# First attention of a decoder block: rotary products for head pairs, queries and keys in alternate slots

## What is computed

```
q, k, v = complex projections of x, 16 heads x 64
phase = cos(t*om) + i sin(t*om)         # om = [omega, -omega], 32 + 32 frequencies per head
qr, kr = q * phase, k * phase
s  = real(sum_d qr[i,d] * conj(kr[j,d]))
qn, kn = sum_d |q|^2, sum_d |k|^2
E  = exp(-mu * |i-j|)
maha = max(qn[i] + E^2*kn[j] - 2*E*s, 0) / V(E)
logits = coef * log1p(maha / nu) - 0.5*64*log(V), causal
out = softmax(logits) @ v ; y = [real(out), imag(out)] @ Wo
```

## Time and profile before

| | |
|---|---|
| median of 3 runs | 2667.71 us (2659.65 to 2667.91) |
| the profiled execution | 2664.52 us, of which the span of the core is 2662.8 us |
| PE busy | 2141.3 us (80%), 14544 products |
| DVE busy | 1698.4 us (64%) |
| ACT busy | 1213.7 us (46%) |
| POOL busy | 716.1 us (27%) |
| mean granted TensorE clock | 0.91 of full |
| chain that ended last | PE 43%, DVE 37%, issue 13%, ACT 4%, POOL 2% |

### The profile page before, as it was taken

How to read it: one execution, slowest core, us unless ns; L and a number is a source line. 1 busy time by engine, 2 the same in 40 slices (tenths; PEclk the granted TensorE clock), 3 DMA queues, 4 the chain that set the end, 5 groups by cost and what they waited for, 6 DMA issues and landing times.

```text
span 2662.8 us, 41353 instructions
## 1 busy us (share of the span) xinstructions
PE 2141.3 (80%) x14544; PEld 1454.7 (55%) x14544; DVE 1698.4 (64%) x3952; ACT 1213.7 (46%) x2950; POOL 716.1 (27%) x647
## 2 busy tenths in 40 slices
PE   2885888689887888679887888679887888688687
PEld 1554466546664566546664566546664566555344
DVE  8976972689346972679356972679346972623444
ACT  2551575246632574236632575236632574233233
POOL 0541540135201540135201540135201540100000
PEclk8996999899997999799997999899987999788799
DMA  4000000000000000000000000000000000020000
GB/s 173 1 2 15 1 1 9 1 17 1 9 1 2 17 1 9 1 18 1 9 1 2 17 1 9 1 18 1 9 1 2 17 1 9 1 79 1 9 16 16
DMA packets 17371, 33.08 MB, mean 12 GB/s; under 512 B 2735, under 2 KB 8887, under 8 KB 16391
## 3 DMA queue, kind: packets, MB, share of 16 engines
q1 hardware_dynamic: 15718, 25.61, 2.8%
q0 software_dynamic: 1440, 4.72, 0.5%
HBM read 24.03 MB, written 5.77 MB: 11 GB/s over the span
## 4 chain that ended last, share of the span: by engine, by line
PE 43%; DVE 37%; issue 13%; ACT 4%; POOL 2%; DVEq 0%; ACTq 0%; SPq 0%; DMA 0%; POOLq 0%
PE bank L1138 41%; DVE work L414 11%; DVE bank L423 5%; DVE work L412 3%; DVE work L432 3%; ACT work L788 2%; PE bank L1142 2%; DVE max L655 2%; POOL work L1048 1%; POOL work L1060 1%; DVE norm_x_st L357 1%; DVE act_row L367 1%; POOL work L1055 1%; DVE acc L578 1%; DVE negmax L434 1%
## 5 line engine op out<-in xcount | busy, mean ns | idle before, releaser
L1138 PEld LDWEIGHTS bank<-work 128*128 128x128 f32 (+2 forms) x5152 | 377.0, 190 | 182.9 <-issue 155.6
L1138 PE MATMUL bank<-work 128*128 128x128 f32 (+2 forms) x5152 | 407.1, 296 | 64.7 <-DMA work<-in_wo 34.7
L788 ACT ACTIVATE work<-bank 128x512 f32<-128x512 f32 (+1 forms) x560 | 244.6, 516 | 260.6 <-PE bank L1138 246.6
L414 DVE TENSOR_TENSOR work<-bank,table_space 64x512 f32<-64x512 f32 x512 | 352.1, 688 | 6.8
L1138 PEld LDWEIGHTS bank<-sb_w_down,hid 128*128 128x128 f32 x2304 | 287.9, 198 | 89.1 <-issue 52.3
L1138 PE MATMUL bank<-act_T,sb_w_up 128*128 128x512 f32 x576 | 292.6, 631 | 33.9 <-ACT hid L788 18.9
L788 ACT ACTIVATE hid<-bank,sb_b_up 128x512 f32<-128x512 f32 x288 | 193.3, 686 | 252.8 <-PE bank L1138 246.7
L1138 PE MATMUL bank<-sb_w_down,hid 128*128 128x128 f32 x2304 | 289.9, 281 | 16.8 <-DVE acc L578 16.8
L578 DVE SCALAR_TENSOR_TENSOR acc<-bank,wexp,acc 128x128 f32<-128x128 f32 x224 | 63.5, 343 | 356.8 <-PE bank L1138 356.5
L1048 POOL TENSOR_TENSOR work<-work 128x512 f32<-128x512 f32 x128 | 163.4, 1276 | 402.3 <-DVE work L414 307.0
L788 ACT ACTIVATE work<-work 128x512 f32<-128x512 f32 x336 | 196.0, 619 | 153.5 <-DVE work L497 101.1
(11 more groups left out here) (245 smaller groups left out, 3252.2 us busy)
## 6 DMA issues: line engine op xcount, KB each, us to landing
sb_w_up<-in_w_up SPq DMA_DIRECT2D x1, 2304.0 KB
sb_w_down<-in_w_down SPq DMA_DIRECT2D x1, 2304.0 KB
x_T<-in_x_T POOLq DMA_DIRECT2D x9, 256.0 KB, 3.0
x_row<-in_x_row POOLq DMA_DIRECT2D x9, 256.0 KB, 3.1
ctx_T<-in_ctx_T SPq DMA_DIRECT2D x8, 256.0 KB, 2.6
work<-in_ctx_row SPq DMA_DIRECT2D x8, 256.0 KB, 2.9
out<-act_row SPq DMA_DIRECT2D x8, 256.0 KB, 2.3
x_scratch<-act_row SPq DMA_DIRECT2D x7, 256.0 KB, 2.1
```

What stands on the lines that cost most here:

```text
L414: last = v.tensor_tensor(rows(wk[i + 1][o]), rows(src[p]), sinT[o, s].unsqueeze(1).broadcast_to([DH0, GB, N]), ALU.mult)
L788: return nc.scalar.activation(o, i, f, **k)
L1138: return nc.tensor.matmul(o, l, r, start=start, stop=stop, skip_group_check=True)
```

## The change

Two heads form a pair. A bank now holds one part (real or imaginary) of one projection for both heads, 64 + 64 channels, and a slot handles the queries of a pair (even slots) or its keys (odd slots). DVE makes four products of 128 partitions a slot: real x cos, real x sin, imaginary x sin, imaginary x cos. POOL makes real = first - third and imaginary = second + fourth. Both DVE waits at the start of a slot become one for the whole rotation of the slot before. The tables of cosines and sines hold 8 pairs and not 16 heads. Norm sums go to one bank for both slots of a pair; they are transposed and copied once a pair, and both diagonals and both scores of a pair are made in the odd slots. A score is 1 product of 512 columns and 8 of 128 columns with 64 rows each. Three banks (4, 5, 6) hold scores; the transposed probabilities share bank 2 with the values. Everything after the norms is a slot later, ACT copies the norms after the exponentials, and DVE makes the logits of an older head before the Mahalanobis form of a younger one. `DRAIN` goes from 17 to 18. The expert banks become 3 and 5 for 3 and 4.

```diff
-cosT, sinT, dec, dec_inv, wgt, bias_t = (... 16 heads each ...)
+cosT, sinT = (... PR = 8 pairs each ...)
+turned = [wk[4:8], [table_space[:, H0*N + i*W : H0*N + (i+1)*W] for i in range(4)]]
...
-DRAIN = H0 + 1
+DRAIN = H0 + 2
...
 # DVE, slot s
-for i, sm, dn in ((0, q_proj, q_parts), (2, k_proj, k_parts)):
-    if i and rotated: rotated()
-    src = bank[i // 2]
-    if s > 0: dve.wait_ge(qk_rot, tally(g, d, 2 * H0, 2 * s - 1 + i // 2))
-    dve.wait_ge(sm, n(s + 1))
-    v.tensor_tensor(rows(wk[i]), rows(src), bc_h(cosT, s), ALU.mult)
-    for o, p in half:
-        last = v.tensor_tensor(rows(wk[i + 1][o]), rows(src[p]), sinT[o, s]..., ALU.mult)
-    last.then_inc(dn, 1)
-h = s - 2: maha ; h = s - 3: logits
+if s > 0: dve.wait_ge(qk_rot, tally(g, d, 2 * H0, 2 * s))
+dve.wait_ge(re_proj, n(s + 1))
+v.tensor_tensor(rows(wk[0]), rows(bank[0]), bc_h(cosT, s // 2), ALU.mult)
+v.tensor_tensor(rows(wk[1]), rows(bank[0]), bc_h(sinT, s // 2), ALU.mult).then_inc(re_parts, 1)
+if rotated: rotated()
+dve.wait_ge(im_proj, n(s + 1))
+v.tensor_tensor(rows(wk[2]), rows(bank[1]), bc_h(sinT, s // 2), ALU.mult)
+v.tensor_tensor(rows(wk[3]), rows(bank[1]), bc_h(cosT, s // 2), ALU.mult).then_inc(im_parts, 1)
+h = s - 4: logits ; h = s - 3: maha
...
 # ACT, slot s (i = s - 1)
+if i odd: square(i)
 exponentials of head s - 5
+if s odd: act.wait_ge(norms, ...); fn(nrm[:, p % 2], bank[3]...)      # p = (s - 3) // 2
+if i even: square(i)
 copy of values (s - 6); copy of transposed probabilities (s - 7)
+if i odd: act.wait_ge(norm_sums, n(i + 1)); fn(norm_rows, bank[3]...)
 fn(score_bank(h), score_bank(h), ACT.Ln, bias=1.0)                     # h = s - 3
...
 # POOL, slot s
+if s odd: wait norms_sb, score; two diagonals of pair p
+wait im_parts; wk[0] - wk[2] -> re ; wk[1] + wk[3] -> im
 scaling of head s - 6
...
 # PE
+def scores_of(p, g, d):
+    qk = turned[p % 2]
+    S = [score_bank(2 * p), score_bank(2 * p + 1)]
+    pe.wait_ge(diag_done, n(2 * p + 1))
+    mm(S[0][:], dec[:, 2 * p], wk[22][:], stop=False)
+    for b in range(GB):
+        for c in range(2):
+            for u in range(2):
+                ur = slice(DH0 * u, DH0 * u + DH0)
+                mm(rows(S[u])[:, b], rows(qk[c][ur])[:, b], rows(qk[2 + c][ur])[:, b], ...)
+    pe.wait_ge(diag_done, n(2 * p + 2))
+    mm(S[1][:], dec[:, 2 * p + 1], wk[10][:], start=False).then_inc(score, 1)
...
 # PE's order in slot s
+norms_of (s odd) ; project(s) ; values_of(s - 6) ; add_head(s - 8) ;
+scores_of((s - 3) // 2) (s odd) ; transpose_probs(s - 7) ; norm_sums_of(s - 1) ; half_expert(s - DRAIN)
```

More of the change, by code:

```diff
@@ L27 @@
 H0, DH0 = 16, 64
+PR = H0 // 2
 H1, DH1 = 8, 16
@@ L305, in _ @@
             PI = 3.1415925
-            for h in range(H0):
+            for h in range(PR):
                 last = v.tensor_scalar(ang[:, h], tramp[:], res["freq"][:, h:h + 1], None, ALU.mult)
@@ L435, in attn0_slot @@
                                     negate=True).then_inc(logits, 1)
+                h = s - 3
+                if 0 <= h < H0:
+                    M = rows(score_bank(h))
+                    dve.wait_ge(norms_sb, tally(g, d, PR, h // 2 + 1))
+                    dve.wait_ge(score, n(h + 1))
+                    for b in range(GB):
+                        last = v.scalar_tensor_tensor(M[:, b], dec_inv[:, h], nrm[:, h // 2 % 2, h % 2, 0, b:b + 1],
+                                                      M[:, b], ALU.mult, ALU.add)
+                    link(last)
+                    v.scalar_tensor_tensor(M, M, 0.0, bc_h(wgt, h), ALU.min, ALU.mult).then_inc(maha, 1)
             def attn0_sum(g, d):
@@ L842, in attn0_slot @@
                     last.then_inc(exped, 1)
-                if 0 <= s - 1 < H0 - 1:
-                    square(s - 1)
-                h = s - 5
+                p = (s - 3) // 2
+                if s % 2 == 1 and 0 <= p < PR:
+                    act.wait_ge(norms, tally(g, d, PR, p + 1))
+                    fn(nrm[:, p % 2], bank[3][:, 2 * N:4 * N].rearrange("p (t r u w) -> p u t r w", t=2, r=4, u=2)[:, :, :, :, 0],
+                       ACT.Copy).then_inc(norms_sb, 1)
+                if 0 <= i < H0 and i % 2 == 0:
+                    square(i)
+                h = s - 6
                 if 0 <= h < H0:
@@ L921, in heads_and_experts @@
                         t_to_T(g, 2, bank[2], d - 2)
-                for s in range(DRAIN, H0 + 6):
+                for s in range(DRAIN, H0 + 7):
                     if heads:
@@ L1098, in heads @@
             def heads(g, d, with_tail):
-                for s in range(H0 + 5):
+                for s in range(H0 + 6):
                     attn0_slot(s, g, d)
@@ L1272, in half_expert @@
                         experts_down(j - 1, g, d, heads)
-                for s in range(H0 + 7):
+                for s in range(H0 + 8):
                     if experts and s == 3:
@@ L1600, in tile, with pairs @@
         return c(np.tile(v.reshape(1, -1), (128, 1)))
-    def heads(w, parts):
-        r = w.reshape(D, 2, H0, DH0)
-        return c(np.stack([r[:, p] for p in parts], 2).reshape(D, H0, len(parts) * DH0))
+    def pairs(w):
+        return c(w.reshape(D, 2, H0 // 2, 2, DH0).transpose(0, 2, 1, 3, 4).reshape(D, H0, 2 * DH0))
     def spread(i_gate, f_gate, shape):
```

221 lines of the change are left out of this document (106 added, 115 removed).

## The result

The changed kernel takes 2744.15 us (median of 4 runs, 2743.52 to 2745.07), the kernel before beside it 2666.01 us (4 runs, 2659.65 to 2667.91): a ratio of 1.030 (95% interval 1.0285 to 1.031), slower by 78 us. The profiled execution took 2743.78 us with a span of 2742.1 us and a mean granted clock of 0.902. The forecast was 2712 us, slower by 47. Direction and range hold; of the 78 us the forecast has 47, so 31 are missing.

What follows compares the result with a forecast made beforehand. DVE bounds the kernel before, PE close behind; after the change a cycle over two slots does. 2664.5 + 57 (attentions, mostly their later ends) - 9 (setup) = 2712 us, chance 0.55; range 2645 to 2795, the forecast's own 2685 to 2740.

Steps and rivals of the forecast that it cites:

- DVE's slot: DVE's work in a slot: two of six rotation instructions go, so 7.60 us becomes 6.2.
- the sum: The prediction's added durations: 15.6 us for the two-slot cycle, attention landmarks, and 2664.5 + 57 - 9 = 2712 us in total.
- PE's load: PE's own work per pair of slots: 14.1 us, with 2.08 us for the sixteen 64-row products.
- The cycle over two slots: Dependency loop through DVE, ACT, POOL and PE: 15.6 us a pair against 15.2, costing 2 us an attention.
- The start: First slots of an attention: slot 6 at the same time as before, slot 14 at 105.8 us against 104.4.
- The walk through slots 4 and 5: At an attention's start: slots 4 and 5 already run in the two-slot cycle, 15.1 us without transposes.
- 1 us with a bound of 4: PE's lower clock after idling ahead of an attention's last scores: 0.5 to 4 us counted, 1 taken.
- The end: End of an attention: first expert product 7.1 us later, 138.8 against 131.7 from slot 0; +7 us a group.
- The setup: Before the first attention: DVE's angle work and its reduction to sine and cosine halve, saving 9.3 us.
- Rival 1: Steady slots: the cycle is slack and PE's load binds, 14.1 us a pair; 2635 us in total, chance 0.2.
- Rival 2: End of an attention: the cycle holds but the later end is absorbed; 2672 us in total, chance 0.14.
- Rival 3: 64-row products do not overlap or wait for banks, +1.5 us a pair; 2809 us, chance 0.11 shared with a fourth rival.

Runs made afterwards that it cites:

- e1: The changed kernel with ACT's copy of the norms moved ahead of the exponentials in odd slots; 2659.0 us, 0.998 of the kernel before.
- e3: The changed kernel with PE projecting the next even slot's real part ahead of transposes and norm sums; 2764.6 us, 1.037 of the kernel before.
- e6: The changed kernel with extra unused 512-column products on PE ahead of its diagonal waits in slots 3, 5, 7 and 17; 2695.1 us.
- e2: The changed kernel with ACT's copy of the norms moved to the even slot's end, ahead of the logarithm; 2632.7 us, 0.988 of the kernel before.
- e9: The changed kernel with the sixteen 64-row products ordered head by head, not interleaved; 2948.2 us, 1.107 of the kernel before.
- e8: The changed kernel with DVE's Mahalanobis form ahead of the logits, as in the kernel before; 2687.0 us, 1.008 of the kernel before.

## Why the prediction was right in sign and short in size

**DVE's slot: 0.5 us too long.** 6.2 us were predicted. The rows give 5.72 (from 657.59 to the next slot's first product at 663.31), since instructions of 128 partitions that stand back to back are 0.60 us apart (657.59, 658.20), not the 0.68 from start to start that I had taken: four products 2.40 us, and the way from the first of them to the logarithm 5.67 us, where the sum has 6.1.

**PE's load: right.** The sixteen 64-row products take 1.98 us for 2.08 (the other figure that I weighed was 2.3), and a pair without its waits for others 15.31 - 0.72 - 0.51 = 14.1, as predicted; where PE sets the pair itself, in e1, it is 13.8.

**The cycle over two slots: right in kind, 0.3 too long.** 5.67 on DVE, 2.28 from the logarithm to the diagonal (predicted 2.4), 1.09 on POOL (1.1), 6.27 on PE until DVE's next product (6.1): 15.31 for 15.6. The 0.4 us too much on DVE and 0.2 too little on PE partly cancel. e1 shows the cycle by taking its ACT part away. What was missing is the branch over the transposes and ACT's copy, 0.3 us from being the longest, which e3 brought out.

**The start: the step that failed.** I had slot 6 "at the same time as before"; it comes 2.0 us later, and slot 8 at 62.7 for 58.8. The walk through slots 4 and 5 gave 15.1 us, and at full clock that is what they take: 14.9 in e6 (1798.9 to 1813.77), 16.8 in the change (1213.17 to 1229.98). I had not asked what PE does in slot 5: it has neither values nor transposes yet, waits 4.98 us and comes back at half clock into the scores, which stand on the cycle. That the clock falls after a wait stood in my text for the end only, at 1 us with a bound of 4. In e6 the clock of slots 5, 7 and 17 gives 5.2 us a group. With 1 counted, 4.2 are missing, 29 us over seven groups, and the periods are 4.1 us longer than forecast (11.1 for 7.0, by the means of the table of runs); the other 2.6 of the 31 us came with the setup and the first attention (1.6 us later, where the sum had 1 earlier). That the two sizes fit so well is partly luck, since smaller errors cancel: all that stands ahead of the first expert product was summed 0.8 us too long (138.8, in e6 138.0).

**The end: right place, too short.** First expert product 11.5 us later for 7.1. Of the 4.4 between, 2.8 stand at slot 14 already, and the other 1.6 are the clock in slot 17 (3.50 for 2.06 us): in e6 slot 14 to the first expert product takes 32.9 us, where the sum has 33.0. PE's wait of 2.10 us, which was to go, shrank only: the second pair of expert products now waits 1.52 us for ACT, whose first expert activation now has the last head's logarithm ahead of it. From the first expert product on the group of the table is 1.1 us shorter than before, where the sum had 0.1.

**The setup: right, 7.4 for 9.3.** Half the angles' work is gone; the start of the first attention is then held by POOL, with waits of 2.60 us, which the sum had not.

**Rival 1, PE as the bound, 2635 us.** Wrong for the change as made, but e2 is this rival: with one copy moved, PE is the bound, the pair lasts 14.33 us and the time is 2632.7. The reason given against it (ACT's order is written out) was the right one. **Rival 2** fell: nothing absorbed the later end. **Rival 3** fell in the change; e9 is its case, and shows that its price, 97 us, was counted without the clock: e9 takes 204 us more than the change.

What stays open: the 1.8 us a group that e6 gains behind the first expert product and the 2.4 us that e8 gains there, and why e2 gains 26 us more than e1 in detail; the traces show that most of it lies in slots 4 to 6, where e1 still waits 3.46 us in slot 5 and comes back at the low clock, and e2 waits 2.05 us and does not.

## What to carry to other kernels

When a change takes work from the bounding engine and also regroups steps, write the new cycle down through every engine's queue, all branches, with their spare time, before counting the relief; the cheapest repair is often the place of one small copy in one queue. Test the relief alone in the old order: it tells what the regrouping costs. And read the first and last slots of a software pipeline by themselves: an engine that has not got all its work there waits longest there, and on PE such a wait can be paid twice, once as idle time and once in the clock.

## What the runs showed of the hardware

- In slots 5, 7 and 17 of the change, PE's waits of 4.98, 2.90 and 2.19 us were followed by the clock of 1.2 GHz, and 64-row products that take 2.06 us at 2.4 GHz took 3.06 to 3.50. The length of the wait alone does not tell: 2.16 us in slot 3 were followed by full clock in the change and by the low clock in e2, 2.05 us in slot 5 of e2 by full clock. Useless products in these waits gave 49 us of 2744 back, and nothing where the waits were short already (2617.2 against 2613.4).
- 32 instructions of 64 rows take 1.98 us when the two halves of the array alternate, each with its own bank, and 3.42 us when one half's come first and then the other's. Half of 3.42 would be 1.71, so by this estimate entering and leaving the form costs 0.27 us at most.
- DVE instructions of 128 x 512 fp32 that take 0.68 us start 0.60 us apart when nothing is between them (657.59 and 658.20); in the kernel before, with instructions of 64 partitions among them, it was 0.68 (626.62 and 627.30).
